# A decoder layer on one core: context and weights handed over already turned, weight products moved beside the first batch, and another order of steps

## The reference

```
x = x + attn(layernorm(x))              # 16 heads of 32: q, k, v = x @ W.T; softmax; @ Wff.T + bff
x = x + xattn(ctx, ctx, layernorm(x))   # one head of 512 over the 750 context rows:
        # softmax((x @ Wq.T + bq) @ (ctx @ Wk.T).T / sqrt(512)) @ (ctx @ Wv.T + bv) @ Wo.T + bo
h = layernorm(x)                        # router: scores of 2048 keys, the best 8, softmax of these,
x = h + gate * sum(w_k * values[idx_k]) # weighted rows of a 2048 x 512 table; the gate needs
                                        # the mean over all batches of log(1 + variance)
```

## Time and profile before

| | |
|---|---|
| median of 3 runs | 3028.26 us (3023.71 to 3029.1) |
| the profiled execution | 3032.06 us, span 3030.2 us |
| mean granted TensorE clock | 0.961 of full |
| TensorE matmul busy | 2773.7 us, 92% of the span |
| VectorE, ScalarE, GpSimd busy | 2162.0, 1498.3, 740.0 us |
| moved by DMA | 280.40 MB, mean 93 GB/s |

### The profile page before, as it was taken

The page is one execution under the profiler, slowest core; times in us unless marked ns, Lnnn a source line. Parts: engine busy times, 40 slices in busy tenths (PEclk is TensorE's granted clock), DMA queues, the critical chain, the costliest instruction groups (busy, mean ns, idle before and its releaser), DMA issues.

```text
span 3030.2 us, 56150 instructions
## 1 busy us (share of the span) xinstructions
PE 2773.7 (92%) x18911; PEld 2092.0 (69%) x18911; DVE 2162.0 (71%) x4148; ACT 1498.3 (49%) x4403; POOL 740.0 (24%) x619
## 2 busy tenths in 40 slices
PE   8699999999999999999999999999999999999500
PEld 4567777777777777777777777777777777776300
DVE  3445777877777777887777777777777777786543
ACT  1346555555555555555555555555555555554200
POOL 0001222222222222222222222222222223232310
PEclk8899999999999999999999999999999999999755
DMA  4101222322222222222222222232222222222299
GB/s 151 39 22 42 70 92 81 92 84 84 84 75 88 70 85 87 87 87 83 82 80 85 72 81 87 87 93 78 87 85 77 74 76 88 86 88 82 76 324 312
DMA packets 106523, 280.40 MB, mean 93 GB/s; under 512 B 14401, under 2 KB 14449, under 8 KB 102481
## 3 DMA queue, kind: packets, MB, share of 16 engines
q1 hardware_dynamic: 57842, 147.71, 15.4%
q0 software_dynamic: 40960, 117.47, 13.4%
q10 hardware_dynamic: 7680, 14.68, 1.3%
HBM read 235.77 MB, written 44.04 MB: 92 GB/s over the span
## 4 chain that ended last, share of the span: by engine, by line
PE 73%; DVE 12%; issue 6%; ACT 3%; SPq 3%; DMA 2%; DVEq 1%; POOL 0%; ACTq 0%
PE psX L874 30%; PE psA L874 19%; PE psA L883 6%; PE psF L874 6%; PE psX L883 5%; PE psA L934 4%; ACT pa L487 3%; PE psA L957 2%; DVE top L764 2%; SPq L386 2%; SPq L387 1%; DVE nmax L697 1%; DMA agg_scratch<-agg 1%; DVE idx L767 1%; DVE stats_A L609 1%
## 5 line engine op out<-in xcount | busy, mean ns | idle before, releaser
L427 POOL DMA_INDIRECT vg<-in_L_ffn_aux_values,idx x512 | 494.6, 966 | 1744.3 <-DVE agg L789 972.0
L487 ACT ACTIVATE pa<-psA,nmax 112x224 f32<-112x224 f32 x1024 | 443.7, 448 | 194.5 <-DVE nmax L697 191.0
L789 DVE SCALAR_TENSOR_TENSOR agg<-vg,wt,agg 112x512 f32<-112x512 f32 x448 | 395.7, 883 | 18.0 <-DMA vg<-in_L_ffn_aux_values,idx 8.9
L874 PE MATMUL psX<-big,gT 128*112 128x375 f32 x1024 | 336.2, 480 | 2.3 <-ACT nx L526 1.8
L697 DVE TENSOR_REDUCE nmax<-psA 112x4 f32<-112x896 f32 x256 | 266.8, 1084 | 99.6 <-PE psA L934 99.6
L874 PE MATMUL psX<-pT,cx 125*128 125x224 f32 x1536 | 304.9, 355 | 0.0
L874 PEld LDWEIGHTS psX<-pT,cx 125*128 125x128 f32 x1536 | 286.1, 190 | 3.9
L710 DVE TENSOR_TENSOR pa<-pa,rsum 112x896 f32<-112x896 f32 x256 | 279.5, 1092 | 9.5 <-DVE rsum L708 0.3
L874 PEld LDWEIGHTS psX<-big,gT 128*112 128x112 f32 x1024 | 177.4, 176 | 132.1 <-ACT nx L526 2.4
L451 ACT COPY paT<-psA 112x448 f32<-112x448 f32 x512 | 238.7, 548 | 12.2 <-PE psA L883 7.7
L874 PE MATMUL psX<-wffT,oT 128*112 128x512 f32 x512 | 227.7, 598 | 17.1 <-ACT oT L451 17.1
(11 more groups left out here) (186 smaller groups left out, 5813.8 us busy)
## 6 DMA issues: line engine op xcount, KB each, us to landing
cx<-in_ctx SPq DMA_DIRECT2D x32, 1500.0 KB
xa<-in_x SPq DMA_DIRECT2D x32, 448.0 KB, 5.8
xr<-in_x SPq DMA_DIRECT2D x32, 448.0 KB, 5.0
base_scratch<-x SPq DMA_DIRECT2D x32, 448.0 KB, 3.1
agg_scratch<-agg SPq DMA_DIRECT2D x64, 224.0 KB, 3.3
vg<-in_L_ffn_aux_values,idx POOLq DMA_INDIRECT x512, 3.4
m<-base_scratch SPq DMA_DIRECT2D x8, 448.0 KB, 14.8
m<-agg_scratch SPq DMA_DIRECT2D x8, 448.0 KB, 16.8
```

The source lines that it names most:

```text
L427: pool.indirect_dma_start(vgv[:, c % SLOTS, k, :], None, aux_values, bass.IndirectOffsetOnAxis(ap=idx[:, t, n:n + 1], axis=0))\
L487: last = nc.scalar.activation(pa[:, t, h, :], psA[0:R, h, t * S:(t + 1) * S], ACT.Exp, bias=nmax[:, k % 2, h, t:t + 1], accum_out=rsum[:, ...
L789: last = nc.vector.scalar_tensor_tensor(agg[:, :], vgv[:, c % SLOTS, k, :], w, agg[:, :], ALU.mult, ALU.add)
L874: last = nc.tensor.matmul(dst, stationary, moving, start=n == 0, stop=n == len(pairs) - 1)
```

## The change

The host hands over eight weights already transposed (`_TURNED`) and, beside the context as it was, a second copy `in_ctx_t`, laid out so that each of 128 partitions reads one run of 4 x 750 numbers. This is done in `kernel()` before the launch.

In the kernel:

- Steps X ctx 0 to 3 are gone on TensorE and ScalarE. SP loads `big` from `ctx_t` for the next batch once the second context score of this one is full (`next_cxT`); the untransposed context is still loaded as before.
- The setup's transposes and the copies out of them are gone. ScalarE and VectorE split the first three weights straight from their staging tiles.
- What is left of the setup becomes steps "W", run in iteration 0 only, behind the steps that `SETUP` names. Their products use the banks of X and F, idle in that iteration (`spare`). Waits for their results stand at the first use.
- SP issues the first weight, x, the other weights, the keys and router weights, the output weight and then the small loads, without a wait between; the rest follow as tiles come free.
- `ORDER` is another permutation of the same steps without X ctx. Among its moves: G sum 0 behind A turn; A qk 2 behind A qk 1; X query ahead of A share 0; G sums 5 and 6 together behind X score 1; A qk 3 ahead of A mix 0; F scores later; X out 1 behind A mix 3.

```diff
 ORDER = (
-    ("A", "norm", 0), ("G", "sum", 0), ("X", "enter", 0), ("A", "turn", 0), ("X", "ctx", 0), ("X", "ctx", 1),
-    ("X", "norm", 0), ("G", "sum", 1), ("A", "qk", 0), ("A", "value", 0), ("X", "turn", 0), ("A", "score", 0),
-    ("G", "sum", 2), ("A", "share", 0), ("F", "norm", 0), ("X", "query", 0), ("A", "prob", 0), ("A", "qk", 1),
-    ("X", "ctx", 2), ("A", "qk", 2), ("G", "sum", 3), ("F", "turn", 0), ("X", "ctx", 3), ("A", "score", 1),
-    ("X", "score", 0), ("A", "share", 1), ("F", "route", 0), ("X", "score", 1), ("F", "learn", 0), ("A", "mix", 0),
-    ("G", "sum", 4), ("A", "qk", 3), ("F", "score", 0), ("X", "prob", 0), ("A", "prob", 1), ("X", "prob", 1),
-    ("F", "score", 1), ("G", "sum", 5), ("A", "score", 2), ("X", "mix", 0), ("A", "mix", 1), ("A", "share", 2),
-    ("G", "sum", 6), ("A", "prob", 2), ("F", "top", 0), ("X", "mix", 1), ("A", "score", 3), ("X", "out", 0),
-    ("F", "score", 2), ("A", "mix", 2), ("F", "score", 3), ("A", "share", 3), ("A", "prob", 3), ("G", "sum", 7),
-    ("F", "top", 1), ("X", "out", 1), ("A", "mix", 3),
+    ("A", "norm", 0), ("X", "enter", 0), ("A", "turn", 0), ("G", "sum", 0), ("X", "norm", 0), ("A", "qk", 0),
+    ("A", "value", 0), ("X", "turn", 0), ("G", "sum", 1), ("A", "score", 0), ("G", "sum", 2), ("X", "query", 0),
+    ("A", "share", 0), ("F", "norm", 0), ("A", "prob", 0), ("A", "qk", 1), ("A", "qk", 2), ("G", "sum", 3),
+    ("F", "turn", 0), ("X", "score", 0), ("A", "score", 1), ("G", "sum", 4), ("A", "share", 1), ("F", "route", 0),
+    ("X", "score", 1), ("G", "sum", 5), ("G", "sum", 6), ("A", "qk", 3), ("A", "mix", 0), ("X", "prob", 0),
+    ("F", "learn", 0), ("A", "prob", 1), ("X", "prob", 1), ("F", "score", 0), ("A", "score", 2), ("X", "mix", 0),
+    ("A", "mix", 1), ("A", "share", 2), ("A", "prob", 2), ("F", "score", 1), ("A", "score", 3), ("X", "mix", 1),
+    ("F", "top", 0), ("F", "score", 2), ("A", "share", 3), ("A", "mix", 2), ("X", "out", 0), ("G", "sum", 7),
+    ("A", "prob", 3), ("F", "score", 3), ("F", "top", 1), ("A", "mix", 3), ("X", "out", 1),
 )
...
+SETUP = {("A", "norm"): (("W", "split", 0),),
+         ("A", "turn"): (("W", "keys", 0), ("W", "keys", 1), ("W", "keys", 2), ("W", "keys", 3)),
+         ("A", "value"): (("W", "route", 0), ("W", "m2", 0)),
+         ("A", "score", 0): (("W", "m2", 1), ("W", "m2", 2), ("W", "m2", 3), ("W", "router", 0)),
+         ("A", "score", 1): (("W", "cb", 0), ("W", "m1", 0), ("W", "m1", 1)),
+         ("A", "score", 2): (("W", "m1", 2), ("W", "m1", 3), ("W", "gb", 0))}
...
+        def spare(n):
+
+            return (psX, psF)[n // 2 % 2][:, n % 2, :]
...
+            def next_cxT(b, t):
+                if t == 0 or (isinstance(b, int) and b == B - 1):
+                    return
+                wait_full(sp, "X", FILL["X", "score", 1] + 1, b)
+                sp.dma_start(big[:, :], row(ctx_t, b + 1)).then_inc(cxT_loaded, 16)
...
             pool.wait_ge(small_loaded, 16 * SMALL)
-            pool.wait_ge(setup_drained, FILLED)
...
-            def ctx_turned(b, c):
-                for half in range(2):
-                    j = FILL["X", "ctx", c] + half
-                    copy_out("X", j, b, cxT[:, c, half * HK:(half + 1) * HK], bank("X", j)[:, 0:HK])
...
+            def split_hi(*_):
+                for n, w in enumerate((wqT, wkT, wvT)):
+                    act.wait_ge(weight_loaded[n], 16)
+                    for c in range(C):
+                        nc.scalar.activation(w[0][:, c, :], staged[n][:, c, :], ACT.Copy,
+                                             scale=float(D) ** -0.5 if n == 0 else 1.0).then_inc(setup_hi, 1)
+                act.wait_ge(small_loaded, 16 * SMALL)
...
+            def split_lo(*_):
+                for n, w in enumerate((wqT, wkT, wvT)):
+                    for c in range(C):
+                        dve.wait_ge(setup_hi, C * n + c + 1)
+                        nc.vector.scalar_tensor_tensor(w[1][:, c, :], staged[n][:, c, :],
+                                                       float(D) ** -0.5 if n == 0 else 1.0, w[0][:, c, :].bitcast(F32),
+                                                       ALU.mult, ALU.subtract).then_inc(split, 1)
+                dve.wait_ge(small_loaded, 16 * SMALL)
+                nc.vector.tensor_copy(bv_rows, bvc[:, :].unsqueeze(2).to_broadcast([P, C, R])).then_inc(small_step, 1)
...
+            def router_split(*_):
+                dve.wait_ge(mask_loaded, 16)
+                dve.wait_ge(setup_drained, KEYED)
+                dve.wait_ge(const_ready, 2)
+                nc.vector.tensor_copy(rkS[:, :], rk32).then_inc(keys_split, 1)
+                dve.wait_ge(keys_split, 1)
+                lo(rkL[0:RD + 1, :], rk32[0:RD + 1, :], rkS[0:RD + 1, :]).then_inc(keys_split, 1)
...
-            def ctx_turn(b, c):
-                if c == 0:
-                    pe.wait_ge(ctx_loaded, 16 * (b + 1))
-                for half in range(2):
-                    j = FILL["X", "ctx", c] + half
-                    wait_free(pe, "X", j, b)
-                    for k in range(3):
-                        last = turned(bank("X", j)[:, k * KP:(k + 1) * KP], cxv[:, 3 * half + k, c * P:(c + 1) * P])
-                    filled("X", j, last)
...
+    a = np.asarray(inputs["ctx_1024"]).reshape(B, KP, KC, C, P).transpose(0, 4, 3, 2, 1)
+    arrays["in_ctx_t"] = a = np.ascontiguousarray(a).reshape(B, P, C * SK)
```

More of the change, by code:

```diff
@@ L243, in wait_drained, with with_setup @@
             wait(eng, drained[s][j % banks[s]], nth(s, j, b) + 1)
+        def with_setup():
+            for at in ORDER:
+                yield at
+                yield from SETUP.get(at, ()) or SETUP.get(at[0:2], ())
         def pipeline(eng, step):
             def iteration(i):
-                batch = {"A": i, "X": i - 1, "F": i - 2, "G": i - 3}
-                for s, name, arg in ORDER:
+                batch = {"A": i, "X": i - 1, "F": i - 2, "G": i - 3, "W": 0}
+                for s, name, arg in with_setup() if isinstance(i, int) and i == 0 else ORDER:
                     b = batch[s]
@@ L369, in store_agg @@
                     sp.dma_start(tiles(row(agg_dram, b))[:, t, :], agg[:, :]).then_inc(agg_stored, 16)
-            pipeline(sp, {("X", "mix"): next_ctx, ("A", "turn"): next_x, ("X", "enter"): next_xr,
+            pipeline(sp, {("W", "split"): after_split, ("W", "keys"): after_keys, ("W", "router"): after_router,
+                          ("W", "cb"): first_cxT, ("W", "gb"): first_ctx,
+                          ("X", "score"): next_cxT, ("X", "mix"): next_ctx, ("A", "turn"): next_x, ("X", "enter"): next_xr,
                           ("F", "norm"): store_base,
@@ L918, in value @@
             def value(b, _):
+                if isinstance(b, int) and b == 0:
+                    pe.wait_ge(split, 3 * C)
                 wait_drained(pe, "A", FILL["A", "turn", 0] + 1, b)
@@ L1060, in place @@
             def place():
-                wait(pe, setup_drained, fills[0] - banks["A"] + 1)
+                wait(pe, setup_drained, fills[0] - 3)
                 fills[0] += 1
-                return psA[:, (fills[0] - 1) % banks["A"], :]
-            def turn_weight(w):
-                for i in range(C):
-                    dst = place()
-                    for o in range(C):
-                        last = turned(dst[:, o * P:(o + 1) * P], w[:, o, i * P:(i + 1) * P])
-                    last.then_inc(setup_full, 1)
@@ L1092, in _ @@
-            turned(place()[:, 0:RD], rw).then_inc(setup_full, 1)
-            pe.wait_ge(setup_drained, fills[0])
-            dst = place()
-            for i in range(C):
-                last = product(dst[:, i * RD:(i + 1) * RD], [(qw[:, i * P:(i + 1) * P], rwT[:, 0:RD])])
-            last.then_inc(setup_full, 1)
-            for n in range(4):
-                dst = place()
-                for k in range(4):
-                    last = turned(dst[:, k * P:(k + 1) * P], keys[:, 4 * n + k, :])
-                last.then_inc(setup_full, 1)
@@ L1103, in _ @@
-            pe.wait_ge(setup_drained, fills[0])
-            for n in range(4):
-                product(place()[0:RS, :], [(rwT, keysT[:, n * BANK:(n + 1) * BANK])]).then_inc(setup_full, 1)
-            dst = place()
-            for i in range(C):
-                last = turned(dst[:, i * P:(i + 1) * P], uw1[:, i * P:(i + 1) * P])
-            last.then_inc(setup_full, 1)
-            pe.wait_ge(setup_drained, FILLED)
-            pipeline(pe, {("A", "turn"): turn("A", "turn", xa, normed(xa_normed)),
+                return spare(fills[0] - 1)
@@ new lines, in make_gb @@
+            def make_gb(*_):
+                dst = place()
+                for i in range(C):
+                    last = product(dst[:, i:i + 1], [(xwk[:, e, i * P:(i + 1) * P], bqc[:, e:e + 1]) for e in range(C)])
+                last.then_inc(setup_full, 1)
+            pe.wait_ge(const_ready, 1)
```

(3 more changed lines are left out.)

240 lines of the change are left out of this document (124 added, 116 removed).

## The result

The changed kernel took 2929.41 us (median of four runs, 2921.48 to 2931.37) where the kernel before took 3028.68 us on the same chip: a ratio of 0.9667, 95% interval 0.9643 to 0.9692. The prediction was 2928 us. The profiled execution was the quickest of the four, 2921.48 us with a span of 2919.7 us, while its counterpart of before was among the slower ones. So the two spans differ by 110.5 us, the two medians by 99.3.

A forecast was written before the change was run, and what follows sets the result against it. TensorE's queue was taken as the bound: 2.36 us a batch times 31 gives 73 us, plus 27 from the start, 100 us off, so 2928 us; its own range 2905 to 2955, 8 in 10 for 2893 to 2976.

The forecast's parts named there:

- the start: Before the loop: first projection at 25 us, X enter of the second iteration at 112, 27 us earlier (bounds 12 and 38).
- the end: Last iterations, 33rd and 34th: some -3 to +5 us, taken as 0; the closing part not touched.
- The handover: A turn to first projection: without ctx 0 and 1 only 0.31 of 2.00 us a batch come back; the rest becomes idle.
- Ctx 2 and 3: Context transposes later in each batch: nothing waits in their place, so removing them gives 1.44 us.
- X out 1: Between last mixing and X enter: covers TensorE's 0.55 us wait for ScalarE's copy, plus 0.06 us between steps, each batch.
- The narrow places on VectorE: Before A turn, 0.3 us of room, and after the second context score, 0.7 us: both counted as costing nothing.
- rival 2: VectorE takes over in a narrow place, or gathers land late; at 1.5 us a batch, 2974 us; 22 in 100.
- The second context load: The added 1500 KB load each batch, issued a good 60 us before it is wanted: counted as costing nothing.
- the products inside the first batch: Weight products moved from ahead of the first batch into it: 37 us, partly filling idle stretches, taken as 25 us net.
- the router's split: First batch, third softmax idle: gives nothing, because VectorE splits the router's keys there before it divides.
- The clock: Rival: the new idle after A turn drops TensorE's clock to 1.2 GHz each batch, giving 3185 us; 5 in 100.
- the idle of 1.79 us: Argument against the slow clock: an idle at 182.13, as long as the new one, left the clock at 1.00.

The follow-up runs named there:

- e1: The changed kernel with the step order of before, its context steps left out; 3013.21 us, 0.9846 of the kernel before.
- e2: The changed kernel, new order, with the context turned on TensorE again and no second context load; 2996.9 us, 0.9798 of the kernel before.
- e3: The kernel before with only the new start (turned weights, weight products inside the first batch), old order and context steps kept; 3036.09 us, 0.9916 of the kernel before.
- e9: The changed kernel with X out 1 ahead of A mix 3 again; 2940.37 us, 0.9614 of the kernel before.
- e7: The changed kernel with the turned context loaded for the first batch alone, the other 31 loads left out; 2923.93 us, 0.9558 of the kernel before.
- e6: The changed kernel with G sum 0 between X enter and A turn; 3029.23 us, 0.9896 of the kernel before.
- e4: The changed kernel with the next batch's x normalised ahead of F top 1 and X enter cut in two around A turn; 2895.35 us, 0.9462 of the kernel before.
- e11: e4 with the first iteration's router split behind A share 0, and G sum 1 moved behind A score 0; 2897.24 us, 0.9463 of the kernel before.
- e10: The kernel before, unaltered, traced on a chip where it is slower; one run, 3065.53 us.

## Why the prediction was right, and where its terms were off

**The frame held.** TensorE's queue set the time, a period read from its timeline times 31 plus a start gave it, and the sum came within 0.1% of the median. The period was put at 82.6 and is 82.34 us; the start's gain at 27 and is 24.8; the end's at 0 and is 4.3. That the median was hit to 1.4 us is in part luck: the terms were read from one pair of executions, and in that pair the gain is 110.5 us, not the 100 of my sum. The medians lie nearer to each other than the pair, by 11 us, and that cancelled the miss.

**The handover, 0.31 us.** I put the distance from A turn to the projection at 2.49 us; it is 2.41, with the idle at 1.43 (1.5 to 1.7 forecast), released by VectorE's subtraction as said. So this term is 0.39 us. With the two below it makes 2.44 of the 2.59 us from A turn to A turn; the other 0.15 were not assigned to a step. The bare handover of the first batch was the right row to read.

**Ctx 2 and 3, 1.44 us.** The sum is right, the reason given for it was short. I wrote that nothing waits in their place. That is true in the new order, where the context scores and A qk 2 stand ahead of A score 1; e1 shows that in the old one the scores of A wait 1.42 us there, as much as was removed. The loop's gain is therefore not 1.75 us of context and 0.61 of order side by side, as my sum has it: e1 to e3 give 0.71 for the context steps in the old order and 2.28 in the new, with the reservations named there.

**X out 1, 0.61 us.** The idle before X enter is gone, and e9 puts it back: 0.54 us of period, 13.6 us of time. This term holds by itself.

**The narrow places on VectorE, nothing.** The forecast of 0.3 and 0.7 us of room cannot be read off the trace directly, but no wait of A turn for x and none of the F transposes for a bank comes in the loop, so rival 2 did not happen.

**The second context load, nothing.** e7 shows it.

**The start, 27 us.** The first projection came at 26.17 (25 forecast) and X enter at 114.37 (112), so the products inside the first batch cost 25.9 us net (25 forecast). That the router's split would stand in A share's way was seen, and it is the 5.45 us ahead of A prob 0. e3 measures the start at 23.5 us.

**The clock, 5 in 100.** It stayed at its upper level, and the argument from the idle of 1.79 us was sound as far as it reached. e6 shows how far that is: with the same steps and a gap of 3.04 us the clock falls in every batch, and the gain over the kernel before would nearly be gone, 1% in place of 4.3% in that group. What keeps the changed kernel clear of this is that no gathered rows are added between VectorE's part of X enter and its subtraction. The old place of G sum 0, ahead of both, would have done as well: in e1 the idle is 1.54 us and the clock stays up. I had also argued that transposes hold the clock. The loop does not separate this: in e6 the stretch without anything but transposes or idle is 4.02 us, in the changed kernel 2.41, in the kernel before 2.80. The start of the kernel before does. Its TensorE begins with transposes at 6.60 and does nothing else until 19.5:

```profile
6.60 3.65 PE L883 MATMUL psA<-ident,cx 128*128 128x128 f32 x16 [6.60 <-DMA cx<-in_L_attn_Wq]
10.04 2.28 PE L883 MATMUL psA<-ident,m 128*128 128x128 f32 x16
```

The first 16 come every 0.21 us. From 10.20 on they come every 0.11 us, and the trace has the granted clock at 1.00 from 10.14 on. So here the clock rose behind transposes alone. The Trainium skill ("TensorE: Matmul & The Clock Gate", Part 4) says that the full rate does not engage for transposes; these rows disagree, and the prediction was right to go by the trace.

**Left open.** Why VectorE's first maxima start 1.38 us later on some chips, and what a gap between the 1.43 us that left the clock up and the 3.04 us that did not would do.

## What to carry to other kernels

A step on the bounding engine that covers a handover is worth only what is left when that handover lies bare. Before it is taken out, ask for each place what will stand there instead; here the removal gave 0.71 us in the old order and 2.28 us in the new. A gap on TensorE has two prices, its length and the clock beside it: 1.43 us cost only itself, 3.04 us cost another 1.80 us or more through the clock. Work of TensorE that is ready (here half of X enter) put between a short product and its reader takes such a gap away altogether; with the earlier norm that goes with it, this was worth 1.1% in e4.

## What the runs showed of the hardware

VectorE and GpSimd stand in each other's way. An add of gathered rows takes VectorE 0.75 us, but one in each batch takes 2.6 to 2.8 us, in all kernels in which GpSimd's `x<-x,cb` runs at that moment. The changed kernel, GpSimd and VectorE:

```profile
1031.13 2.40 POOL L456 TENSOR_TENSOR x<-x,cb 112x1024 f32<-112x1024 f32 x1 [1.95 <-DVE nx L672]
```

```profile
1031.49 3.37 DVE L820 SCALAR_TENSOR_TENSOR agg<-vg,wt,agg 112x512 f32<-112x512 f32 x2
```

Two adds take 3.37 us beside GpSimd's operation and 1.53 us elsewhere in the same batch; with the adds moved away, in e11, none of 173 in a millisecond of the loop is above 0.754. VectorE's slow add, 2.58 us long, ends at 1034.07, only after GpSimd has ended at 1033.53. The Trainium skill ("SBUF — State Buffer", "SBUF: two separate sides") says that the two share a port pair, which one instruction holds to its end, and that a VectorE operation with two inputs in SBUF needs it. The rows agree: the two operations overlap for 2.04 us until GpSimd ends, and the add is 1.83 us longer than 0.75. In the kernel before, where one add starts 0.17 us ahead of `x<-x,cb`, GpSimd's operation takes 2.83 us in place of 2.40.

The kernel before takes 1% more on three of the four chips, at the same granted clock, and nearly all of it appears behind one late start on VectorE in each batch (e10). The changed kernel, which has no idle of VectorE at that place, does not. The cause is open; an idle there is not enough for it (e11).
